# Routed adapters, two layers on one core: the first eviction ahead of h's transposes, and item 0 taken before the order of pairs is known

## The chip, the cores and the metric

One core of one Trainium2 chip. The metric is the device time of one execution in microseconds (us), as the median of several runs; a lower time is better. One further execution is recorded by the hardware profiler, and all rows come from it.

## What is computed

Two layers of the same form act on 128 items of 128 rows and 1024 columns (all fp32). Each item has a role, 1 or 2 of 3 possible, and the role picks the adapter, the same index in both layers:

```
h = x @ W_down[role] + b_down[role]      # 1024 -> 512
h = gelu(h)                              # exact
u = h @ W_up[role] + b_up[role]          # 512 -> 1024
y = x + u
out = (y - mean(y)) * rsqrt(var(y) + 1e-5) * gamma[role] + beta[role]
```

The output of layer 0 is the input of layer 1.

## The kernel before

**Order of the work.** The items are sorted by adapter (that of item 0 first) and taken two at a time, so a pair shares its weights. A layer has 65 pairs, the two layers 130, and the program counts them through. At the start VectorE computes the order of the items (`c_ord`), the adapter of each pair (`c_q`) and its kind (`c_kind`: 0, the same adapter as the pair before; 1 or 2, a new one) from the roles. `s_ctl` and `s_kind` tell the other engines that these are written.

**Arithmetic.** Each fp32 operand is split into a high part (type fp32r, a copy on ScalarE: `xh`, `wdh`, `wuh`, `hh`) and a low part (the difference, on VectorE: `xl`, `wdl`, `wul`, `hl`). A product is then three matmuls: high by high, high by low, low by high. The down product of an item is 8 x 3 matmuls into a bank `pD[e]`, e being the item of the pair. The up product of a pair is done on both items at once, by a scheme of seven half-size products (Strassen's) into the banks `bX` (two, in turn) and `bZ`. The combinations of h that it needs are GpSimd's `sums` (`cs`), those of the weights VectorE's `factors` and one more subtraction (L881).

**A step, software-pipelined.** In step i the engines work on pair i (down), w = i-2 (h of that pair is prepared) and u = i-3 (up product, evictions, the layer norm's sums); the norm's last parts and the store belong to i-4. TensorE's order in a step (L541 to L569) alternates: product 0 of u, a quarter of the down product of i, product 1, a quarter, and so on to product 6 and the last two quarters. Each product waits for the eviction of the bank that it adds to (`s_v`), for its weights (`s_wu`) and its half of h (`s_hl`). Product 2 waits for the first eviction of u.

An eviction on VectorE adds a bank to half an item's row tile in `xt` (`onto`, L943, the first three; `last_onto`, L951, the last four, which also sum the rows). ScalarE seeds each bank with the bias before the products add to it (`seed_d`, `seed_x`, `seed_z`) and applies gelu. h goes through DRAM (`store_h`, `load_h` on SP's queue), comes back in blocks as `hq` and is transposed in blocks of 32 by VectorE into `hT` (`transpose_h`, L918). In layer 1, x comes back from DRAM in the same manner (`transpose_x`, L904).

**Each engine's program** is a list of `begin(i)` and `end(i)`, written out for the first steps and those at a layer's change, and otherwise a loop over six steps whose body begins with `end(i-1)`, so the jump back lies between a `begin` and an `end`. Work that belongs to a new adapter stands in a conditional block (`kinds.when_new`, `when_near`, `when_far`), which is jumped over where the kind says so.

**VectorE's begin(i)** (L1004) is, in order: read of a kind, the two `transpose_h` of w, first eviction of u, with new down weights their second half of low parts (`take_wd_1`), low part of x of item 1 (`low_x`), second eviction, `low_h` 0, third eviction, with new up weights their last three low parts (`take_wu_2`), variance, the two `scale` (L974), fourth eviction, transpose of x, fifth eviction, with a new adapter for w the up bias (`bias`, L865), `low_x` of the next pair's item 0, sixth eviction, mean. **end(i)** (L1040) begins with `take_wu_0` (first two low parts of the up weights), `take_wd_0`, then the remaining `low_h`, the last eviction, and `take_wu_1`.

**ScalarE's end(i)** (L732) issues the loads of weights, then goes through high parts of h, the norm's scaling of u-1 (`normal`), `high_x` and gelu, `take_wu_0` (four high parts), the wait for the down bias (`bias_landed`), the seeds, `take_wd_0`, squares. The load of the down bias itself is SP's (`down_bias`, L301, L411), ahead of its row loads.

**At the start** SP issues the roles, item 0's x, and, once the first adapter is known, the down bias and four chunks of down weights (L392 to L398). ScalarE waits for `s_ctl` and `s_kind` (L577) before anything of item 0. TensorE zeroes the two `pD` banks, then computes sums for the order (L508), then zeroes `bX` and `bZ` (L511).

## Time and profile before

| | |
|---|---|
| runs | 2773.15, 2773.26, 2773.27 us; median 2773.26 |
| profiled execution | 2774.88 us, its span 2773.0 us |
| granted TensorE clock, mean | 0.991 |
| VectorE busy | 2179.8 us (79%) |
| ScalarE busy | 1667.0 us (60%) |
| GpSimd busy | 1382.2 us (50%) |
| DMA engines, mean busy share | some 6 tenths all through, 207 GB/s |
| chain that ended last | TensorE 83%, issue 7%, VectorE 6%, DMA, ScalarE, GpSimd 1% each |

The profile times every instruction of each engine, and names what ended an engine's idle time ("releaser"). "PE" is TensorE's matmul, "PEld" its weight load, "DVE" VectorE, "ACT" ScalarE, "POOL" GpSimd, "SPq" SyncE's queue, which issues most DMAs; "DVEq L895" is a semaphore that VectorE raises at line 895 (`ready`). "issue" stands for idle time in which nothing that the profile shows was awaited. Of a line that is merged from n instructions, the time is that of all n. Matmuls overlap: they start 0.227 us apart and are shown with 0.39.

### The profile page before, as it was taken

Reading aid. Unit: us, or ns where it says so; the run is one execution under the profiler, and the core shown is the slowest. Engines: PE = TensorE matmul, PEld = TensorE weight load, DVE = VectorE, ACT = ScalarE, POOL = GpSimd, SP = SyncE. Lnnn points to the kernel's source line nnn. Section 1 sums busy time; section 2 is a strip of 40 time slices with the busy share of each in tenths; the row PEclk is TensorE's granted clock in tenths of the full one; section 3 lists DMA queues with packets and bytes.
Section 4 is the critical chain, followed back from the end, with each engine's and each line's share of the span. In section 5 each row is a group of like instructions: output and inputs, shape, how many; then the busy total and the mean of one; then the engine's idle time right before and its main releaser. Section 6 shows DMA issues by size and latency. Waiting matters only on the chain.

```text
span 2773.0 us, 54757 instructions
## 1 busy us (share of the span) xinstructions
PE 2688.5 (97%) x11714; PEld 2204.8 (80%) x11714; DVE 2179.8 (79%) x3357; ACT 1667.0 (60%) x2905; POOL 1382.2 (50%) x1050
## 2 busy tenths in 40 slices
PE   8999999999999999999989999999889999999997
PEld 5888888877788888888768888888677888888885
DVE  6777777778777777777888788877788787878887
ACT  4666656666666666656666565665556565566565
POOL 1445555554555555555444454544444554544545
PEclk9999999999999999999999999999999999999999
DMA  6656666666666666666766665665756665666664
GB/s 207 212 200 213 211 204 208 205 223 226 211 213 204 207 208 207 209 204 238 232 190 198 200 220 191 212 208 188 240 178 214 198 218 193 209 207 198 206 208 149
DMA packets 360582, 573.29 MB, mean 207 GB/s; under 512 B 40144, under 2 KB 239952, under 8 KB 359248
## 3 DMA queue, kind: packets, MB, share of 16 engines
q1 hardware_dynamic: 359136, 554.92, 60.9%
q10 hardware_dynamic: 1008, 14.68, 1.4%
q14 instruction: 426, 3.49, 0.4%
q8 instruction: 12, 0.20, 0.0%
HBM read 364.97 MB, written 204.47 MB: 205 GB/s over the span
## 4 chain that ended last, share of the span: by engine, by line
PE 83%; issue 7%; DVE 6%; DMA 1%; ACT 1%; DVEq 1%; POOL 1%; SPq 0%; ACTq 0%; POOLq 0%
PE pD L524 44%; PE bX L536 23%; PE bZ L536 17%; DVE hl L933 1%; DVE xt L951 1%; DVE xT L904 1%; DVE wul L850 1%; DVE xt L943 1%; DVE wdl L831 0%; DMA htok<-hg 0%; DMA cbd<-in_bd 0%; DMA out<-xt 0%; DVEq L258 0%; SPq L387 0%; DVE hT L918 0%
## 5 line engine op out<-in xcount | busy, mean ns | idle before, releaser
L524 PE MATMUL pD<-wdh,xh 128*128 128x512 f32 x2080 | 812.4, 391 | 9.6 <-DVEq L895 9.6
L524 PE MATMUL pD<-wdl,xh 128*128 128x512 f32 x2080 | 811.4, 390 | 0.0
L524 PE MATMUL pD<-wdh,xl 128*128 128x512 f32 x2080 | 811.0, 390 | 0.0
L469 POOL TENSOR_TENSOR xt<-xt,cgb 128x1024 f32<-128x1024 f32 x258 | 620.7, 2406 | 370.4 <-ACT xt L717 370.4
L709 ACT ACTIVATE pC<-xt,nmean 128x512 f32<-128x512 f32 x520 | 358.6, 690 | 288.8 <-DVE nmean L959 280.1
L477 POOL TENSOR_TENSOR cs<-hT 128x256 f32<-128x256 f32 x130 | 97.5, 750 | 828.6 <-DVE hT L918 828.6
L717 ACT ACTIVATE xt<-xt,rstd 128x1024 f32<-128x1024 f32 x258 | 296.5, 1149 | 325.3 <-POOL rstd L455 321.7
L524 PEld LDWEIGHTS pD<-wdh,xh 128*128 128x128 f32 x2080 | 392.1, 189 | 94.0 <-DVEq L895 7.9
L536 PE MATMUL bX<-wuh,hh 128*128 128x512 f32 x1040 | 411.0, 395 | 49.9 <-DVE xt L943 41.5
L524 PEld LDWEIGHTS pD<-wdl,xh 128*128 128x128 f32 x2080 | 392.1, 189 | 81.7
L524 PEld LDWEIGHTS pD<-wdh,xl 128*128 128x128 f32 x2080 | 391.8, 188 | 81.9
L536 PE MATMUL bX<-wul,hh 128*128 128x512 f32 x1040 | 407.5, 392 | 0.0
L536 PE MATMUL bX<-wuh,hl 128*128 128x512 f32 x1040 | 407.3, 392 | 0.0
L933 DVE TENSOR_TENSOR hl<-cs,hh 128x512 fp32r<-128x512 f32 x260 | 287.3, 1124 | 148.1 <-issue 139.8
L699 ACT ACTIVATE hh<-cs 128x512 fp32r<-128x512 f32 x260 | 163.7, 630 | 350.0 <-PE bX L536 258.0
L974 DVE SCALAR_TENSOR_TENSOR xt<-xt,nmean,cgb 128x1024 f32<-128x1024 f32 x260 | 324.2, 1287 | 0.5 <-issue 0.3
L536 PE MATMUL bZ<-wuh,hh 128*128 128x512 f32 x780 | 304.6, 390 | 7.3 <-issue 5.0
L536 PE MATMUL bZ<-wul,hh 128*128 128x512 f32 x780 | 303.8, 389 | 0.0
L536 PE MATMUL bZ<-wuh,hl 128*128 128x512 f32 x780 | 303.7, 389 | 0.0
L452 POOL TENSOR_TENSOR rstd<-var,mhalf 128x2 f32<-128x2 f32 x129 | 218.4, 1693 | 164.2 <-DVE var L966 161.8
L536 PEld LDWEIGHTS bX<-wuh,hh 128*128 128x128 f32 x1040 | 196.5, 189 | 104.3 <-DVE xt L943 51.4
L951 DVE SCALAR_TENSOR_TENSOR xt<-bX,xt 128x512 f32<-128x512 f32 x260 | 177.2, 682 | 104.2 <-PE bX L536 102.7
(105 smaller groups left out, 3834.2 us busy)
## 6 DMA issues: line engine op xcount, KB each, us to landing
xq<-in_xB SPq DMA_DIRECT2D x130, 512.0 KB, 3.5
htok<-hg SPq DMA_DIRECT2D x260, 256.0 KB, 2.8
hq<-htok SPq DMA_DIRECT2D x1040, 64.0 KB, 2.2
xt<-in_x SPq DMA_DIRECT2D x130, 512.0 KB, 4.3
mid<-xt SPq DMA_DIRECT2D x130, 512.0 KB, 3.7
xq<-mid SPq DMA_DIRECT2D x520, 128.0 KB, 3.2
xt<-mid SPq DMA_DIRECT2D x130, 512.0 KB, 4.2
out<-xt SPq DMA_DIRECT2D x128, 512.0 KB, 2.9
```

Source lines behind the costliest of these rows:

```text
L452: eng.tensor_tensor(rstd[:, n:n + 2], var[:, n:n + 2], mhalf[:, 0:1].broadcast_to([128, 2]), ALU.pow)\
L469: eng.tensor_tensor(xt[:, k, :], xt[:, k, :], cgb[:, 1, :], ALU.add).then_inc(s_o, 1)
L477: eng.tensor_tensor(cs[:, 0, :], b1, b2, ALU.add).then_inc(s_S, 1)
L524: last = eng.matmul(pD[e][:, :], a[:, e, 128 * k:128 * k + 128], w[:, k, :], start=False, stop=(k == 7 and n == 2), skip_group_check=True)
L536: last = eng.matmul(bank[:, :], a[:, left, 128 * c:128 * c + 128], w[:, n, c, :], start=(start and c == 0 and m == 0), stop=(c == 1 and m ...
L699: eng.activation(dst, src, ACT.Copy).then_inc(s_hh, 1)
L709: eng.activation(junk[:, :], xt[:, u.slot(e), K * m:K * m + K], ACT.Square, bias=nmean[:, n:n + 1], accum_out=ssq[:, b, m, e:e + 1]).then_ ...
L717: eng.activation(xt[:, k, :], xt[:, k, :], ACT.Copy, scale=rstd[:, n:n + 1]).then_inc(s_z, 1)
L850: eng.tensor_tensor(wul[:, n, :, :], block, wuh[:, n, :, :].bitcast(fp32), ALU.subtract)\
L933: eng.tensor_tensor(blocks, src, high.bitcast(fp32), ALU.subtract).then_inc(s_hl, 1)
L951: eng.scalar_tensor_tensor(out=half(u, e, m), in0=bank[:, :], scalar=1.0, in1=half(u, e, m), op0=ALU.mult, op1=ALU.add, accum_out=ys[:, b, ...
L974: eng.scalar_tensor_tensor(out=xt[:, k, :], in0=xt[:, k, :], scalar=nmean[:, n:n + 1], in1=cgb[:, 0, :], op0=ALU.add, op1=ALU.mult).then_i ...
```

## The change

It moves work and leaves the arithmetic as it is:

- VectorE's `begin(i)`: the first eviction of u stands ahead of the two transposes of h, and the read of a kind behind the low part of x.
- VectorE's `take_wu_0` takes in `bias` and the subtraction that stood in `take_wu_1`. It is called in `begin(i)` where `bias` was, ahead of the low part of the next x and the sixth eviction, and no longer in `end(i)`.
- ScalarE's `take_wu_0` stands earlier in `end(i)`, ahead of `normal`, `high_x` and gelu.
- The load of a new down bias is issued by ScalarE at the head of `end(i)` and no longer by SP.
- Item 0: ScalarE takes its x, bias, seed and first two high parts of the weights ahead of its wait for the order; VectorE takes x's low part before it finishes the order; TensorE zeroes all banks ahead of its sums for the order.

```diff
--- before.py
+++ after.py
@@ -298,11 +298,6 @@
                 s = p.times(2, e - 2 * NP * p.layer())
                 return eng.value_load(c_ord[0:1, bass.ds(s, 1)], min_val=0, max_val=NB - 1)
 
-            def down_bias(p):
-                row = adapter(p)
-                count(eng, s_sd, p + -1, 2, 2)
-                eng.dma_start(cbd[:, :], bd[row, :].broadcast_to([128, K])).then_inc(s_bd, 16)
-
             def up_biases(p):
                 row = adapter(p)
                 count(eng, s_sz, p + -1, 1, 1)
@@ -407,8 +402,6 @@
                 store_h(v, 1)
                 load_blocks(i + 1, 1)
                 load_h(v, 1)
-                if not (i + 1).first():
-                    kinds.when_new(i + 1, down_bias)
                 load_rows(w, 0)
                 load_rows(w, 1)
                 store(z, 0)
@@ -504,13 +497,13 @@
             for bank in pD:
                 last = eng.matmul(bank[:, :], zero[:, 0:128], zero[:, 0:K], start=True, stop=True)
             last.then_inc(s_bits, 1)
+            for bank in bX + [bZ]:
+                last = eng.matmul(bank[:, :], zero[:, 0:128], zero[:, 0:K], start=True, stop=True)
+            last.then_inc(s_bits, 1)
             eng.wait_ge(s_oh, 2)
             eng.matmul(pC[0:1, 0:NSLOT], jf[:, :], oneh[:, :], start=True, stop=True)
             eng.matmul(pC[0:1, NSLOT:2 * NSLOT], rf[:, NB:NB + 1], oneh[:, :], start=False, stop=True,
                        skip_group_check=True).then_inc(s_pc, 1)
-            for bank in bX + [bZ]:
-                last = eng.matmul(bank[:, :], zero[:, 0:128], zero[:, 0:K], start=True, stop=True)
-            last.then_inc(s_bits, 1)
 
             def down(i, e, q):
                 if i.exists():
@@ -574,8 +567,6 @@
         def _(eng):
             eng.wait_ge(s_id, 2)
             eng.activation(gelu_set[:, :], mhalf[:, :], ACT.Gelu)
-            eng.wait_ge(s_ctl, 1)
-            eng.wait_ge(s_kind, 1)
             kinds = Kinds(eng, "ac_kind")
             fd = Phases(eng, "ac_fd", 1)
             fu = Phases(eng, "ac_fu", 1)
@@ -591,6 +582,11 @@
 
             def load_up(p):
                 fetch_up(eng, adapter(p), fu.next())
+
+            def load_bias(p):
+                row = adapter(p)
+                count(eng, s_sd, p + -1, 2, 2)
+                eng.dma_start(cbd[:, :], bd[row, :].broadcast_to([128, K])).then_inc(s_bd, 16)
 
             def bias_landed(p):
                 eng.wait_ge(s_bd, pb.next() * 16 + 16)
@@ -716,6 +712,14 @@
                     count(eng, s_n, p, 2, e + 1)
                     eng.activation(xt[:, k, :], xt[:, k, :], ACT.Copy, scale=rstd[:, n:n + 1]).then_inc(s_z, 1)
 
+
+            high_x(Pair(0), 0)
+            bias_landed(Pair(0))
+            seed_d(Pair(0), 0)
+            take_wd_0(Pair(0))
+            eng.wait_ge(s_ctl, 1)
+            eng.wait_ge(s_kind, 1)
+
             def begin(i):
                 kinds.read(i + 2)
                 kinds.when_new(i, take_wd_1)
@@ -731,23 +735,28 @@
 
             def end(i):
                 u, w = i + -3, i + -2
+                if not (i + 1).first():
+                    kinds.when_new(i + 1, load_bias)
                 kinds.when_near(w, load_up)
                 kinds.when_far(i, load_up)
                 kinds.when_near(i + 1, load_down)
                 kinds.when_far(i + 2, load_down)
                 high_h(w, 1)
+                if not w.first():
+                    kinds.when_new(w, take_wu_0)
                 normal(u + -1, 0)
-                high_x(i + 1, 0)
+                if not (i + 1).first():
+                    high_x(i + 1, 0)
                 gelu(i, 0)
                 high_h(w, 2)
-                if not w.first():
-                    kinds.when_new(w, take_wu_0)
-                kinds.when_new(i + 1, bias_landed)
-                seed_d(i + 1, 0)
+                if not (i + 1).first():
+                    kinds.when_new(i + 1, bias_landed)
+                    seed_d(i + 1, 0)
                 normal(u + -1, 1)
                 seed_x(w)
                 seed_z(w)
-                kinds.when_new(i + 1, take_wd_0)
+                if not (i + 1).first():
+                    kinds.when_new(i + 1, take_wd_0)
                 square(u, 0, 0)
                 square(u, 0, 1)
                 high_h(w, 3)
@@ -803,6 +812,11 @@
             link(eng.tensor_scalar(m1[:, :], io[:, 0:NSLOT], edge, par1, ALU.is_ge, ALU.mult))
             link(eng.tensor_tensor(m0[:, :], m0[:, :], m1[:, :], ALU.subtract))
             eng.tensor_scalar(oneh[:, :], m0[:, :], float(NB - 1), pos, ALU.min, ALU.is_equal).then_inc(s_oh, 1)
+
+            eng.wait_ge(s_xq[0], 16)
+            eng.wait_ge(s_xh, 1)
+            eng.tensor_tensor(xl[:, 0, :], xq[:, 0, :, :].rearrange("p b n -> p (b n)"), xh[:, 0, :].bitcast(fp32),
+                              ALU.subtract).then_inc(s_xl, 1)
             eng.wait_ge(s_pc, 1)
             heads = pC[0:1, NSLOT:2 * NSLOT].rearrange("p (n two) -> p n two", two=2)[:, :, 0]
             eng.tensor_copy(c_ord[:, :], pC[0:1, 0:NSLOT])
@@ -822,7 +836,6 @@
             kinds = Kinds(eng, "ve_kind")
             pd = [Phases(eng, f"ve_pd{g}") for g in range(2)]
             pt = Phases(eng, "ve_pt")
-            pb = Phases(eng, "ve_pb")
             pg = [Phases(eng, f"ve_pu{g}") for g in range(3)]
 
             def low_wd(c, q):
@@ -859,26 +872,23 @@
                 eng.wait_ge(s_sub, c * 4 + 2)
                 eng.tensor_tensor(t4, b21, t2, ALU.subtract).then_inc(s_sub, 1)
 
-            def bias(p):
-                c = pb.next()
+            def take_wu_0(p):
+                c = pg[0].next()
                 eng.wait_ge(s_bu, c * 16 + 16)
                 eng.tensor_tensor(cbu[:, K:H], cbu[:, K:H], cbu[:, 0:K], ALU.subtract).then_inc(s_bz, 1)
-                eng.wait_ge(s_bz, c + 1)
-                eng.sem_inc(s_seen, 1)
-
-            def take_wu_0(p):
-                c = pg[0].next()
                 low_wu(c * 7, 0, b11)
                 low_wu(c * 7, 1, b12)
+                eng.wait_ge(s_wul, c * 7 + 1)
+                eng.tensor_tensor(b11, t2, b11, ALU.subtract).then_inc(s_sub, 1)
                 eng.wait_ge(s_wul, c * 7 + 2)
+                eng.sem_inc(s_seen, 1)
+                eng.wait_ge(s_bz, c + 1)
                 eng.sem_inc(s_seen, 1)
 
             def take_wu_1(p):
                 c = pg[1].next()
                 low_wu(c * 7, 2, t2)
                 low_wu(c * 7, 3, b22)
-                eng.wait_ge(s_wul, c * 7 + 1)
-                eng.tensor_tensor(b11, t2, b11, ALU.subtract).then_inc(s_sub, 1)
                 eng.wait_ge(s_wul, c * 7 + 4)
                 eng.sem_inc(s_seen, 1)
 
@@ -1007,13 +1017,13 @@
                 if (u + -1).last():
                     last_rows(u + -1)
                     return
-                kinds.read(i + 1)
+                onto(u, 1, X, 0, 0)
                 transpose_h(w, 0)
                 transpose_h(w, 1)
-                onto(u, 1, X, 0, 0)
                 kinds.when_new(i, take_wd_1)
                 ready(i, s_wd[1])
                 low_x(i, 1)
+                kinds.read(i + 1)
                 onto(u, 2, bZ, 1, 1)
                 low_h(w, 0)
                 if u.last():
@@ -1031,9 +1041,11 @@
                 last_onto(u, 4, bZ, 0, 1, 3)
                 transpose_x(i + 1, 0)
                 last_onto(u, 5, X, 1, 1, 2)
-                kinds.when_new(w, bias)
+                kinds.when_new(w, take_wu_0)
                 ready(w, s_cb)
-                low_x(i + 1, 0)
+                ready(w, s_wu[0])
+                if not (i + 1).first():
+                    low_x(i + 1, 0)
                 last_onto(u, 6, bZ, 0, 0, 1)
                 mean(u, 0, 6)
 
@@ -1041,8 +1053,6 @@
                 u, w = i + -3, i + -2
                 if (u + -1).last():
                     return
-                kinds.when_new(w, take_wu_0)
-                ready(w, s_wu[0])
                 kinds.when_new(i + 1, take_wd_0)
                 ready(i + 1, s_wd[0])
                 if not only_up(i):
```

## Rows read from the trace of the kernel before

**Rows 1.** The page, part 1: busy time and instructions of each engine.
```profile
PE 2688.5 (97%) x11714; PEld 2204.8 (80%) x11714; DVE 2179.8 (79%) x3357; ACT 1667.0 (60%) x2905; POOL 1382.2 (50%) x1050
```

**Rows 2.** Waits of TensorE: line, for what; us in total, times, longest.
```profile
PE bX L536 <- DVE xt L943: 41.5, 21, 5.7
```

**Rows 3.** Timeline, an ordinary step of layer 0: start, us, engine, line, operation.
```profile
1136.73 0.39 PE L536 MATMUL bX<-wuh,hl 128*128 128x512 f32 x1
...
1136.38 1.30 DVE L918 STREAM_TRANSPOSE hT<-hq 128x512 f32<-128x512 f32 x2
...
1142.59 0.69 DVE L943 TENSOR_TENSOR xt<-bX,xt 128x512 f32<-128x512 f32 x1 [1.43 <-PE bX L536]
```

**Rows 4.** Timeline, a loop turn of layer 1 (VectorE), and TensorE's waits at turns.
```profile
2206.64 0.69 DVE L933 TENSOR_TENSOR hl<-cs,hh 128x512 fp32r<-128x512 f32 x1 [4.86 <-issue]
...
2211.29 1.30 DVE L918 STREAM_TRANSPOSE hT<-hq 128x512 f32<-128x512 f32 x2
...
2214.22 0.67 DVE L943 TENSOR_TENSOR xt<-bZ,xt 128x512 f32<-128x512 f32 x1
...
2213.22 0.50 PE L536 MATMUL bX<-wuh,hh 128*128 128x512 f32 x1 [1.29 <-DVE xt L943]
...
1567.36 0.50 PE L536 MATMUL bX<-wuh,hh 128*128 128x512 f32 x1 [1.29 <-DVE xt L943]
...
2585.50 0.50 PE L536 MATMUL bX<-wuh,hh 128*128 128x512 f32 x1 [1.05 <-DVE xt L943]
```

**Rows 5.** Timeline of the start, and landing of the first weights (by tile).
```profile
13.45 0.28 DVE L820 CUSTOM_DVE_ANT_0 c_kind<-c_new,c_near 1x260 uint16<-1x260 uint16 x1
...
14.97 1.06 ACT L651 ACTIVATE xh<-xq 128x1024 fp32r<-128x1024 f32 x1 [12.69 <-issue]
...
17.52 2.36 DVE L831 TENSOR_TENSOR wdl<-rwd,wdh 128x1024 fp32r<-128x1024 f32 x2 [0.24 <-ACT wdh L605]
...
20.18 0.76 PE L524 MATMUL pD<-wdh,xh 128*128 128x512 f32 x1 [3.69 <-DVEq L895]
...
DMA to landing us min/median/max: 4.5/5.6/6.7
```

**Rows 6.** Timeline, the first up weights.
```profile
52.77 1.23 DVE L911 TENSOR_TENSOR xl<-xq,xh 128x1024 fp32r<-128x1024 f32 x1 [2.92 <-ACT xh L651]
...
64.24 0.50 PE L536 MATMUL bX<-wuh,hh 128*128 128x512 f32 x1 [1.96 <-DVE xt L943]
```

**Rows 7.** Waits of ScalarE, then the timeline, new down weights in layer 1.
```profile
ACT pD L668 <- DMA cbd<-in_bd: 7.8, 2, 6.8
...
1972.37 0.39 PE L524 MATMUL pD<-wdh,xh 128*128 128x512 f32 x1
...
1979.71 2.65 DVE L831 TENSOR_TENSOR wdl<-rwd,wdh 128x1024 fp32r<-128x1024 f32 x2 [8.91 <-ACT wdh L605]
...
1992.44 0.51 PE L524 MATMUL pD<-wdh,xh 128*128 128x512 f32 x1 [1.49 <-DVEq L895]
```

**Rows 8.** Timeline of TensorE, new down weights at the change of layer.
```profile
1336.87 0.39 PE L524 MATMUL pD<-wdh,xh 128*128 128x512 f32 x1
...
1346.69 0.50 PE L536 MATMUL bX<-wuh,hh 128*128 128x512 f32 x1 [1.49 <-DVE xt L943]
...
1349.84 0.50 PE L524 MATMUL pD<-wdh,xh 128*128 128x512 f32 x1 [1.50 <-DVEq L895]
```

**Rows 9.** Timeline, new up weights; last, a stretch: us, PE busy, clock, DMA, GB/s.
```profile
1418.36 0.79 PE L536 MATMUL bX<-wuh,hh 128*128 128x512 f32 x1 [5.67 <-DVE xt L943]
...
1406.29 2.40 POOL L469 TENSOR_TENSOR xt<-xt,cgb 128x1024 f32<-128x1024 f32 x1 [5.54 <-ACT xt L717]
...
1406.68 2.57 DVE L933 TENSOR_TENSOR hl<-cs,hh 128x512 fp32r<-128x512 f32 x1 [0.63 <-DVE wul L850]
...
2035.00:2040.00 5.00, 4.61 (x13) 0.66 0.64 196
```

**Rows 10.** Waits of VectorE: idle time before the low halves of h.
```profile
DVE hl L933 <- issue: 205.5, 244, 5.1
```

## The prediction

> **What bounds the kernel now.** I read the page first: TensorE is busy for 97% of the span [rows 1], so only its idle time, some clock loss and what lies before its first real matmul can be won. The waits come next. Of TensorE's own waits nearly all lie behind one line, the first kind of eviction, VectorE's add of a bank into xt at L943: 41.5 us in 21 waits [rows 2]. The timeline then shows where they are, and they fall into three kinds.
>
> The ordinary step has none. In layer 0 the last matmul of product 0 starts at 1136.73, VectorE begins the two transposes of h at 1136.38, and it still idles 1.43 us before its third eviction [rows 3]. A change in that step is worth nothing.
>
> The loop turns of layer 1 are the second kind. VectorE stands still for 4.86 us at the jump back ("issue": nothing that the profile shows is awaited), comes late to the transposes at 2211.29, spends 1.30 us on them and only then does the first eviction, for which TensorE has waited 1.29 us at 2213.22. The same wait is there at eight turns, from 1567.36 to 2585.50; they add up to 9.8 us [rows 4].
>
> The third kind are the start and the steps in which an adapter changes [rows 5 to 9].
>
> **Loop turns.** The change puts the first eviction ahead of the transposes. Its bank is ready long before (product 0 is two groups of matmuls earlier), so at a turn it starts where the transposes did and ends about 2211.3 + 0.67 = 2212.0, when TensorE has just come to it (2213.22 - 1.29 = 2211.9). What is late next is the second eviction: transposes, low half of x and eviction together end where they did, at 2214.22 + 0.67 = 2214.9, and TensorE, coming 12 matmuls (2.9 us) after 2211.9, meets it within 0.1 us [rows 4]. So 8 x (1.2 - 0.1) or **-9.0 us**; the ends are 0 and -9.8. The transposes themselves become later by one eviction, 0.7 us, in layer 1. In layer 0 VectorE arrives 0.35 us before product 0's last matmul has even started, so it waits some 0.8 us and the transposes are 1.5 us later; the 1.43 us of idle time before the third eviction, with smaller idle times before it, take that up [rows 3]. GpSimd's sums, ScalarE's high halves and SP's loads of hq wait for the transposes and slide by the same 0.7 to 1.5 us; all of them are needed only a step later. Cost of the move in the ordinary step: nothing, by this cover.
>
> **Start.** Before, ScalarE takes item 0's x only after the order of pairs: that order is written at 13.45 + 0.28, and the first high half starts at 14.97, 1.24 us on. Bias, weights' high halves and x's low half follow, VectorE's low halves of the weights run 17.52 to 19.88, and TensorE starts at 20.18, 0.30 us behind [rows 5]. After, x, bias and the first two high halves are done while the order is still being worked out; the four weight loads, which SP issues as soon as the first adapter is known, take 4.5 to 6.7 us, and I take the first two chunks as landed when the order is done. VectorE does x's low half before the order is finished (it delays that by 0.1 to 0.3 us) and comes to the weights when the order is done, at 13.9 plus its own entry into the program. I take ScalarE's 1.24 us for that entry: 15.0 + 2.36 + 0.30 = 17.7, or **-2.5 us**. Ends: entry in no time, -3.7; only x's low half saved (1.23 us, [rows 6]), -1.2. The three banks zeroed earlier on TensorE fill time in which it only waited. The first real matmul took 0.76 us against 0.39 later [rows 5, 7], so the clock was low there; it stays so, since an idle stretch precedes it again.
>
> **First up weights.** VectorE now does the first half of pair 0's up weights right behind the bias, in the stretch where it idled 2.92 us before x's low half at 52.77 [rows 6]. The chain from there to the first eviction, for which TensorE waited 1.96 us at 64.24, and on to the last three parts is VectorE's own. It ends 2.9 us sooner: **-2.9 us**, ends 0 and -2.9.
>
> **Middle of layer 1, new down weights.** SP issued the bias late in its queue, and ScalarE waited for it: 7.8 us in two waits, 6.8 of them here [rows 7]. ScalarE's high halves of the weights stood behind, and VectorE idled 8.91 us until 1979.71. Now ScalarE issues the load itself at the head of its half step, some 7 us before the seed needs it; weight loads of twice its size took 4.5 to 6.7 [rows 5]. The 6.8 us are gone. From the matmuls behind product 6 to the third group of down matmuls it took 1992.44 - 1972.37 = 20.1 us here, and 1349.84 - 1336.87 = 13.0 at the change of layer, where the bias was on time [rows 7, 8]. The difference, 7.1, holds some clock loss. I take **-6.6 us**, ends 0 and -7.1. The other wait, 1.0 us in the middle of layer 0, gives **-0.7 us**, since the last seed behind it waits for VectorE anyway; ends 0 and -1.
>
> **Down weights elsewhere.** At the change of layer TensorE waited 1.49 us for the first eviction and 1.50 for the weights' second half [rows 8]. The eviction now comes in time, but the weights' low halves end where they did, so the second wait grows to 3.0: **0 us**. A single idle stretch of that length can cost clock. In 2035 to 2040, behind an idle stretch of 2.5, the granted clock was 0.66 [rows 9], a loss of some 1.6 us. Two steps get such a stretch, and I count one of them: **+1.6 us**, ends 0 and +3.2.
>
> **Up weights (three steps).** TensorE waits up to 5.67 us for VectorE's chain [rows 9]. The chain gets shorter by the transposes (1.3 us). But the first half of the up weights (bias, two low halves, one subtraction) now stands beside GpSimd's two shifts. GpSimd's add from 1406.29 takes 2.40, and VectorE's subtraction of 512 columns issued at 1406.68 takes 2.57 instead of 0.69 [rows 4, 9]: it waited for GpSimd to end. Before, such a block cost this chain 1.9 us once or so; now both shifts lie across it, up to 4.8. The Trainium skill, "SBUF — State Buffer", section "SBUF: two separate sides", says that a VectorE operation with two SBUF inputs and a GpSimd operation exclude each other for a whole instruction; by it alone the step would cost about 2 us more at each of the three. ScalarE's early high halves of the weights also put off x's high half, so that TensorE meets it late, inside a chain that VectorE bounds anyway. I take -0.6 at each, **-1.8 us** in all; ends -3.9 and +6.
>
> **Tail.** The first eviction once leaves the transposes behind, but the rest of the chain stays: **-0.3 us**.
>
> **Sum.** -9.0 - 2.5 - 2.9 - 6.6 - 0.7 + 1.6 - 1.8 - 0.3 = -22.2 us against the profiled execution's 2774.88 (span 2773.0, 1.9 around it): 2752.7. The median of the runs lies 1.6 lower, so 2751.
>
> **Rivals.** (1) *Turns and start only.* The switches are chains of VectorE, ScalarE and GpSimd together; what is won at one point may come back at the next, with the clock down each time. Then -9.0 - 2.5 - 2.9 + 3.2 = -11.2 remain, 2762. For it: the blocks of rows 9. Against it: ScalarE's wait for the bias is named by the profile and has no second cause. (2) *More is won.* All waits at the turns, the start at its near end, the up steps at theirs and no clock loss: -9.8 - 3.7 - 2.9 - 7.1 - 1.0 - 3.9 - 0.3 = -28.7, 2745. (3) *A stall of instruction supply, slower.* A conditional block of five operations is now skipped in the middle of VectorE's begin instead of at the head of end. If that skip stalls once a turn as the jump back does, in the same step, there is no slack under it: 4.86 - 0.6 (an ordinary one) = 4.3 us at some ten turns of layer 1, +43 against -22, so 2794. Below half that price it does not decide. Against it: 244 such idle times add up to 205.5 us, 0.84 on average with the turns among them [rows 10], so skips of blocks as long cost about 0.6. The Trainium skill, "Runtime: NRT & Kernel Launch", section "Instruction fetch mechanics", says that a taken branch whose target lies outside the fetched window stalls; the 4.86 us at the turn fit that. (4) *No change.* If the first eviction still comes late, because something else (product 0, or the stall growing) holds VectorE at the turn, and the bias lands no sooner, only the 5 us of start and first weights remain: 2768.
>
> **Chances.** Forecast 0.6; (1) 0.19; (2) 0.12; (3) 0.04; (4) 0.05. A difference of 0.2%, 5.5 us, is about what a measurement tells from none. Faster by more: 0.91; within: 0.05; slower: 0.04. The range reaches from rival 2 to rival 1, with their margins: 2743 to 2762.
>
> **What would show it.** At the layer 1 turns: first eviction ahead of the transposes, and no wait of 1.1 to 1.3 us at product 2. TensorE's first real matmul at about 17.7. No wait of ScalarE for cbd, and VectorE's low halves in the middle of layer 1 about 6 us sooner. At the up steps the wait of about 5 us split in two, with GpSimd's adds between VectorE's low halves. Wrong would be: the waits at the turns still over 1 us, a VectorE idle time over 1 us at the new skip, or an ordinary step that takes longer than before.

## The result, and the profile after

The kernel after the change takes 2748.98 us (median of 4 runs, 2748.43 to 2749.48) against 2773.2 of the kernel before (4 runs in the same comparison, 2772.51 to 2773.27): the ratio is 0.9913, 95% interval 0.9896 to 0.993. The profiled execution took 2748.52 us, its span is 2746.7, against 2774.88 and 2773.0. The forecast was 2751.0, with a range of 2743 to 2762.

Part 1 of the page of the kernel after, to be read beside [rows 1]:

```profile
PE 2686.8 (98%) x11714; PEld 2207.3 (80%) x11714; DVE 2209.5 (80%) x3357; ACT 1669.8 (61%) x2905; POOL 1388.9 (51%) x1050
```

TensorE's busy time is 1.7 us less, and the span is 26.3 less: idle time went. VectorE is busy 29.7 us longer with as many instructions, some of them drawn out. The waits of the kernel after (engine, tile, line, what was awaited: us in total, times, longest):

```profile
DVE hl L943 <- issue: 161.8, 243, 4.5
...
PE pD L517 <- DVEq L905: 18.9, 7, 5.6
...
PE bX L529 <- DVE xt L953: 8.2, 7, 2.2
PE bX L529 <- DVEq L905: 8.1, 4, 2.5
PE bZ L529 <- issue: 7.6, 4, 3.2
...
ACT pD L664 <- DMA cbd<-in_bd: 3.2, 1, 3.2
```

The first eviction, now L953, kept TensorE waiting 41.5 us in 21 waits [rows 2]; now 8.2 in 7. Part of that came back elsewhere. TensorE's waits for VectorE's low parts ahead of `pD` were these in the kernel before:

```profile
PE pD L524 <- DVEq L895: 9.6, 5, 3.7
```

They are now 18.9 us. The longest is the one at the start in both kernels, 3.7 before and 5.6 now, where TensorE is only ready sooner. ScalarE waits for the down bias once, at the start, instead of the 7.8 us of [rows 7]. The sum called issue was 205.5 [rows 10] and is 161.8; the forecast had not expected that.

The timeline of the kernel after, at the start, the first up weights, the up weights of layer 1, the middle of layer 1, a turn and the last steps (start, us, engine, line, operation):

```profile
13.52 0.28 DVE L834 CUSTOM_DVE_ANT_0 c_kind<-c_new,c_near 1x260 uint16<-1x260 uint16 x1
...
14.42 2.36 DVE L844 TENSOR_TENSOR wdl<-rwd,wdh 128x1024 fp32r<-128x1024 f32 x2 [0.61 <-DVE c_kind L834]
...
17.08 0.76 PE L517 MATMUL pD<-wdh,xh 128*128 128x512 f32 x1 [5.57 <-DVEq L905]
...
60.56 2.89 DVE L863 TENSOR_TENSOR wul<-rwu,wuh 128x1024 fp32r<-128x1024 f32 x2
...
62.33 1.71 POOL L475 TENSOR_TENSOR cs<-hT,cs 128x256 f32<-128x256 f32 x1
...
63.37 1.75 DVE L863 TENSOR_TENSOR wul<-twu,wuh 128x1024 fp32r<-128x1024 f32 x1
...
65.43 0.47 PE L529 MATMUL bX<-wuh,hh 128*128 128x512 f32 x1 [2.51 <-DVEq L905]
...
1393.41 6.82 POOL L462 TENSOR_TENSOR xt<-xt,cgb 128x1024 f32<-128x1024 f32 x2 [2.83 <-ACT xt L713]
...
1393.42 4.56 DVE L863 TENSOR_TENSOR wul<-rwu,wuh 128x1024 fp32r<-128x1024 f32 x2
1397.90 3.42 DVE L882 TENSOR_TENSOR rwu<-twu,rwu 128x1024 f32<-128x1024 f32 x1
...
1403.46 0.50 PE L517 MATMUL pD<-wdh,xh 128*128 128x512 f32 x1 [2.80 <-DVEq L905]
...
1411.07 0.50 PE L529 MATMUL bX<-wuh,hh 128*128 128x512 f32 x1 [1.65 <-DVE xt L953]
...
1958.97 2.69 DVE L844 TENSOR_TENSOR wdl<-rwd,wdh 128x1024 fp32r<-128x1024 f32 x2 [2.47 <-ACT wdh L601]
...
1971.29 0.49 PE L517 MATMUL pD<-wdh,xh 128*128 128x512 f32 x1 [2.47 <-DVEq L905]
...
2182.75 0.69 DVE L943 TENSOR_TENSOR hl<-cs,hh 128x512 fp32r<-128x512 f32 x1 [4.49 <-issue]
...
2187.17 0.68 DVE L953 TENSOR_TENSOR xt<-bX,xt 128x512 f32<-128x512 f32 x1
2187.77 1.29 DVE L928 STREAM_TRANSPOSE hT<-hq 128x512 f32<-128x512 f32 x2
...
2694.96 0.69 DVE L953 TENSOR_TENSOR xt<-bX,xt 128x512 f32<-128x512 f32 x1 [2.08 <-PE bX L529]
...
2719.01 0.76 PE L529 MATMUL bZ<-wuh,hh 128*128 128x512 f32 x1 [3.16 <-issue]
```

Stretches of the kernel after (window, us, busy time and count of each engine, granted clock, DMA share, GB/s):

```profile
65.40:69.90 4.50, 4.47 (x13) 3.58 (x14) 2.27 (x5) 1.64 (x3) 0.00 (x0) 0.62 0.90 269
...
1342.00:1346.00 4.00, 4.00 (x11) 3.13 (x12) 3.97 (x7) 0.64 (x2) 2.82 (x4) 0.57 0.77 222
...
1403.40:1407.40 4.00, 3.94 (x10) 3.13 (x11) 3.54 (x7) 3.08 (x7) 0.00 (x0) 0.57 0.05 18
...
1971.30:1976.00 4.70, 4.36 (x18) 3.29 (x19) 4.59 (x7) 0.63 (x1) 3.45 (x4) 1.00 0.89 274
...
2719.00:2724.60 5.60, 5.59 (x13) 4.43 (x14) 2.23 (x7) 3.14 (x6) 4.12 (x2) 0.50 0.24 97
```

Both kernels issue the same matmuls, so the same matmul can be looked up in both traces. How much earlier or later it starts, taken from one place to the next, is what each place won or lost:

| place | forecast | measured |
|---|---|---|
| start | -2.5 | -3.7 |
| first up weights | -2.9 | -0.65 |
| middle of layer 0, down weights | -0.7 | -1.8 |
| middle of layer 0, up weights | -0.6 | -0.9 |
| change of layer, down weights | 0 and clock +1.6 | +0.2 |
| layer 1, first up weights | -0.6 | -0.7 |
| eight turns of layer 1 | -9.0 | -12.9 |
| middle of layer 1, down weights | -6.6 | -6.7 |
| middle of layer 1, up weights | -0.6 | -2.4 |
| last steps | -0.3 | +2.8 |
| sum | -22.2 | -26.8 |

(The forecast's last term for the up weights, -1.8, is split over its three steps. Of the span's 26.3 us 0.4 is rounding and the very end.)

### The profile page after: what moved, and what is told of

The parts are those of the page before. It is cut to its first block, busy times and chain, and to the rows that moved or that the text cites. A ratio compares the mean times of both kernels' runs of the same rounds, so it can differ in the third digit from the quotient of the medians.

```text
span 2746.7 us, 54496 instructions
## 1 busy us (share of the span) xinstructions
PE 2686.8 (98%) x11714; PEld 2207.3 (80%) x11714; DVE 2209.5 (80%) x3357; ACT 1669.8 (61%) x2905; POOL 1388.9 (51%) x1050
## 4 chain that ended last, share of the span: by engine, by line
PE 88%; DVE 6%; issue 4%; ACT 1%; DVEq 1%; POOL 0%; DMA 0%; ACTq 0%; POOLq 0%; SPq 0%
PE pD L517 47%; PE bX L529 23%; PE bZ L529 18%; DVE wul L863 1%; DVE xt L961 1%; DVE hl L943 1%; DVE xT L914 1%; DVE wdl L844 0%; DVE xt L953 0%; DVE xl L921 0%; DVE hT L928 0%; DVE xt L984 0%; ACT wdh L601 0%; ACT pC L705 0%; DMA xt<-in_itok 0%
## 5 line engine op out<-in xcount | busy, mean ns | idle before, releaser
L517 PE MATMUL pD<-wdh,xh 128*128 128x512 f32 x2080 | 813.2, 391 | 18.9 <-DVEq L905 18.9
L462 POOL TENSOR_TENSOR xt<-xt,cgb 128x1024 f32<-128x1024 f32 x258 | 629.1, 2439 | 348.7 <-ACT xt L713 348.7
L470 POOL TENSOR_TENSOR cs<-hT 128x256 f32<-128x256 f32 x130 | 154.0, 1185 | 907.4 <-DVE hT L928 907.4
L943 DVE TENSOR_TENSOR hl<-cs,hh 128x512 fp32r<-128x512 f32 x260 | 302.9, 1184 | 103.4 <-issue 96.8
L953 DVE TENSOR_TENSOR xt<-bX,xt 128x512 f32<-128x512 f32 x260 | 178.9, 688 | 149.6 <-PE bX L529 147.1
```

Source lines behind the costliest of these rows:

```text
L462: eng.tensor_tensor(xt[:, k, :], xt[:, k, :], cgb[:, 1, :], ALU.add).then_inc(s_o, 1)
L470: eng.tensor_tensor(cs[:, 0, :], b1, b2, ALU.add).then_inc(s_S, 1)
L517: last = eng.matmul(pD[e][:, :], a[:, e, 128 * k:128 * k + 128], w[:, k, :], start=False, stop=(k == 7 and n == 2), skip_group_check=True)
L943: eng.tensor_tensor(blocks, src, high.bitcast(fp32), ALU.subtract).then_inc(s_hl, 1)
L953: eng.tensor_tensor(half(u, e, m), bank[:, :], half(u, e, m), ALU.add).then_inc(s_v, 1)
```

## The experiments

### One part undone at a time

**e1_undo_evict.** The first eviction stands behind the two transposes again:

```diff
-                onto(u, 1, X, 0, 0)
                 transpose_h(w, 0)
                 transpose_h(w, 1)
+                onto(u, 1, X, 0, 0)
```

> The changed kernel with one edit: the first eviction stands behind the transposes of h again. Theory (the eviction's place carries the loop turns): the eight waits of 1.1 to 1.3 us for the first eviction at the turns of layer 1 are back, and cost with TensorE's restart some 1.6 us each, 13 us; single waits at steps with a new adapter add 1 to 4; the tail gives 2.8 back. About 2761 to 2765, against 2749 for the changed kernel. Rival (the turns were won by the block of up weights that left the head of the half step behind the jump back): the turns stay without waits, 2749 to 2753.

Measured: 2755.96 us (2753.35 to 2756.6), ratio 0.994 [0.9924, 0.9957]; that is 7.0 above the kernel after, between the two expectations. Its timeline:

```profile
1398.19 1.22 DVE L882 TENSOR_TENSOR rwu<-twu,rwu 128x1024 f32<-128x1024 f32 x1
...
1398.25 3.40 POOL L462 TENSOR_TENSOR xt<-xt,cgb 128x1024 f32<-128x1024 f32 x1 [1.07 <-ACT xt L713]
...
1410.59 0.50 PE L529 MATMUL bX<-wuh,hh 128*128 128x512 f32 x1 [4.64 <-DVE xt L953]
...
1557.65 0.50 PE L529 MATMUL bX<-wuh,hh 128*128 128x512 f32 x1 [1.38 <-DVE xt L953]
```

The waits at all eight turns are back. Matmul by matmul it loses 5.3 us on the kernel after over the first four turns (1421 to 1929) and 6.8 from 2061 to 2563; of these, 5.0 belong to the other four turns, and the rest to a wait of 2.32 behind the new up weights (2067.29). It loses 2.2 in the middle of layer 0. But it wins 1.2 at the first up weights, 3.4 and 3.6 where layer 1 takes new up weights, and 2.3 in the last steps. (The execution in this trace was the fastest of the four, 4.8 us above the profiled one of the kernel after.) The L882 row shows why at one of these: there the subtraction takes 1.22 us and GpSimd's second add starts behind it (3.40 long); with the eviction first, GpSimd's two adds follow each other without a gap (6.82 for both) and the same subtraction takes 3.42. Moving one eviction changed which of the two engines came first.

**e2_undo_bias.** SP issues the down bias again (`down_bias`, with `kinds.when_new(i + 1, down_bias)` ahead of `load_rows`), ScalarE's `load_bias` is gone.

> The changed kernel with one edit: SP issues the load of a new down bias again, ahead of its row loads. Theory: ScalarE waits again some 7 us for cbd in the middle of layer 1 and 1 us in the middle of layer 0, of which 6.6 and 0.7 reach TensorE: about 2756. Rival (VectorE's chain there is as long anyway, since the eviction and the up weights moved too): 2749 to 2751.

Measured: 2758.75 us (2756.81 to 2762.63), ratio 0.9947 [0.9931, 0.9964], 9.8 above the kernel after. From its timeline:

```profile
1328.58 0.60 ACT L671 ACTIVATE pD<-cbd 128x512 f32<-128x512 f32 x1 [2.47 <-DMA cbd<-in_bd]
...
1968.42 0.60 ACT L671 ACTIVATE pD<-cbd 128x512 f32<-128x512 f32 x1 [8.60 <-DMA cbd<-in_bd]
...
1970.67 0.77 PE L536 MATMUL bX<-wuh,hh 128*128 128x512 f32 x1 [6.07 <-issue]
```

ScalarE's wait is back, longer than the 6.8 of [rows 7], and TensorE's with it. So the load's late issue is the cause of that wait. Matmul by matmul this run loses 9.3 us on the kernel after in the middle of layer 1, where the change had won 6.7 and where ScalarE's wait is now 1.8 us longer than before the change. It loses 2.7 at the change of layer, where a new wait of 2.47 stands (1328.58). In the middle of layer 0 it loses nothing: there the bias lands in time here too. So this run says nothing on the 1.8 us that the change won there. It also loses 2.3 us over the eight turns, although VectorE's program is the same as in the kernel after. (The execution in this trace was the slowest of the four, 14.1 us above the profiled one of the kernel after, where the medians are 9.8 apart.)

**e3_undo_start.** Item 0's x is taken behind the order of pairs again, on all three engines (`eng.wait_ge(s_ctl, 1)`, `eng.wait_ge(s_kind, 1)` ahead of ScalarE's first work, no early `xl`, the last three banks zeroed behind the sums for the order).

> The changed kernel with the start undone: ScalarE waits for the order before item 0, VectorE takes the low half of its x after the order, TensorE zeroes the last three banks after its sums for the order. Theory: TensorE's first real matmul is at 20.2 instead of 17.1, and all the rest is shifted by that and no more: about 2752.5. Rival (the first up weights set the end of this stretch whatever the start): 2749 to 2750, with a shorter wait for the first up weights.

Measured: 2752.73 us (2750.59 to 2753.42), ratio 0.9929 [0.9912, 0.9945], 3.7 above the kernel after: the time that was expected. In its trace the first real matmul starts at 19.43 and not at the 20.2 expected, 2.35 later than 17.08. (That execution took 2750.59 us, the shortest of the four, and is only 2.1 us above the profiled one of the kernel after.)

**e4_undo_wu.** VectorE's `bias` and `take_wu_0` are two blocks again, the second at the head of `end(i)`, the subtraction is back in `take_wu_1`, and ScalarE's `take_wu_0` stands behind `high_h` 2.

> The changed kernel with the first half of the up weights put back on both engines (bias alone in begin, the two low halves at the head of end, the subtraction with the second half; ScalarE's four high halves behind the high half of h). Theory (locks between GpSimd's shifts and VectorE cost what the shorter chain gives): 2747 to 2751, VectorE's subtraction without the 3.4 us of the changed kernel. Rival A (the new place is worth the 2 to 3 us by which the shift grew at these steps): 2752 to 2755. Rival B (the new place only costs): under 2746.

Measured: 2753.01 us (2751.87 to 2754.09), ratio 0.9928 [0.9911, 0.9944], 4.0 above the kernel after: rival A. The waits of VectorE in it:

```profile
DVE hl L947 <- issue: 206.6, 243, 5.2
```

That is the sum of the kernel before. Matmul by matmul against the kernel after, it loses 2.0 us from 1421 to 1932 and 1.3 from 2070 to 2565, stretches that hold turns and no new weights at all (its trace is 5.6 us longer in sum). This led to the runs with a block added or taken away below.

The four parts undone cost 7.0 + 9.8 + 3.7 + 4.0 = 24.5 us together, against 24.2 that the change brought. That they add up so well is partly chance, as the next run shows.

**b1_evict_only.** The kernel before, with the eviction (and the read of a kind) moved and nothing else.

> The kernel before with one part of the change alone: the first eviction ahead of the two transposes of h, and the read of the next item's kind behind the low half of x. Theory (the eviction's 12.9 us at the eight turns of the loop are its own, and it gives back some 6 us in the tail, at the change of layer and at the first up weights, since undoing it in the kernel after cost only 7 us): 5 to 9 us below the kernel before, 2764 to 2768. Rival (its loss at the weights came only together with the moved low parts, so alone it wins the whole of the turns): 11 to 14 us below, 2759 to 2762.

Measured: 2768.16 us (11 runs, 2764.33 to 2772.25) against 2773.34 (15 runs), ratio 0.9981 [0.9971, 0.999]: 5.2 us won, at the lower end of the theory. Its timeline:

```profile
1561.78 0.69 DVE L933 TENSOR_TENSOR hl<-cs,hh 128x512 fp32r<-128x512 f32 x1 [4.83 <-issue]
```

Its eight turns give 8.6 us against the kernel before, the 9.0 of the forecast to 0.4. The rest of the 12.9 goes with VectorE's idle time at the turns (here 4.4 to 5.2 us in layer 1, 4.90 on average at the eight; in the kernel after 4.06 to 4.49, 4.30 on average). It gives back some 2 us up to the first steps of layer 1, where TensorE now also waits at turns of layer 0 (204.75, 450.63 and 954.27, 0.57 to 0.79 us), and 2.5 in the last steps.

### Can the rest be had?

**c1_tail.** In the last steps, those without down products, the transposes come first:

```diff
-                onto(u, 1, X, 0, 0)
+                if not only_up(i):
+                    onto(u, 1, X, 0, 0)
                 transpose_h(w, 0)
                 transpose_h(w, 1)
+                if only_up(i):
+                    onto(u, 1, X, 0, 0)
```

> The kernel after the change, with the first eviction again behind the two transposes in the last steps alone, those in which no down product is left. In the trace of the kernel after the change TensorE loses 2.8 us more in those steps than before the change (3.16 at 2703.68 and again 3.16 at 2719.01, with a low clock behind the second). Theory (VectorE waits there for product 0, whose eviction now stands ahead of the transposes of h, and so hands the halves of h over late): the two waits of 3.16 go back to those of the kernel before, and the time is some 2.8 us below the kernel after, 2746 to 2747. Rival (the tail is late by the up weights and by GELU, whatever VectorE's order): the waits stay and the time stays at 2748.5 to 2749.5.

Measured: 2747.76 us (2747.16 to 2748.72), ratio 0.9907 [0.9892, 0.9922], 1.2 below the kernel after. In the timeline:

```profile
2703.06 0.47 PE L529 MATMUL bZ<-wuh,hh 128*128 128x512 f32 x1 [1.84 <-issue]
...
2711.84 0.50 PE L529 MATMUL bX<-wuh,hh 128*128 128x512 f32 x1 [3.09 <-DVE xt L953]
```

The waits of 3.16 are 1.84 (as before the change) and 1.21, so VectorE's order was their cause; but a new one of 3.09 for the first eviction stands between them, with a low clock behind it (1.46 there in the kernel before). Matmul by matmul 2.0 of the 2.8 came back; by the medians of the runs 1.2, which is about the scatter.

**c2_wd.** As c1_tail, and `take_wd_1` ahead of the transposes, behind the first eviction.

> As c1_tail, and in the other steps VectorE's take_wd_1 (the second part of the down weights' low parts, only in steps with new weights) stands ahead of the two transposes of h and behind the first eviction. Theory (the low parts of the new down weights end last before TensorE's wait at the change of layer, 2.47 at 1342.00, and before the waits in the middle of the layers, and the transposes of h have time there): the three waits shrink by the 1.3 us that two transposes take on VectorE, the clock does not fall behind the first of them, and the time is 3 to 5 us below c1_tail, 2741 to 2744. Rival (the transposes of h are as urgent as the low parts, since h's product follows): what the weights win h loses, and the time is within 1 us of c1_tail or above it, 2746 to 2748.

Measured: 2746.72 us (2745.87 to 2749.26), ratio 0.9905 [0.989, 0.992]: within 1.1 of c1_tail, so the rival. In the timeline:

```profile
1342.20 0.50 PE L517 MATMUL pD<-wdh,xh 128*128 128x512 f32 x1 [1.76 <-DVEq L905]
...
1345.40 0.50 PE L529 MATMUL bZ<-wuh,hh 128*128 128x512 f32 x1 [1.54 <-DVE xt L953]
```

The wait for the weights shrank from 2.45 to 1.76, and 1.54 came up one product on. One chain of VectorE feeds both.

**c3_lowx.** As c1_tail, and `low_x(i + 1, 0)` ahead of `take_wu_0`.

> As c1_tail, and on VectorE the low half of x for the next item's first down product stands ahead of the low parts of the first up weights (take_wu_0) instead of behind them, which matters in the three steps with new up weights. Theory (TensorE's waits of 1.8, 2.8 and 2.8 us at 673.6, 1403.5 and 2032.2 are for that low half, which is queued behind a subtraction that the shared port draws out to 3.4 us): these waits go, the up weights' own waits behind them grow by less, and the time is 2 to 5 us below c1_tail, 2742 to 2744. Rival (VectorE's work before the first up product is one chain, so what goes at the first wait comes back at the next): the wait moves from the low half to the up weights and the time is that of c1_tail, within 1.5 us.

Measured: 2748.27 us (2747.27 to 2749.28), ratio 0.9908 [0.9892, 0.9923]: nothing, the rival. In the timeline:

```profile
1403.42 1.21 DVE L882 TENSOR_TENSOR rwu<-twu,rwu 128x1024 f32<-128x1024 f32 x1
...
1404.52 0.50 PE L529 MATMUL bX<-wuh,hh 128*128 128x512 f32 x1 [2.69 <-ACT bX L672]
```

The wait of 2.80 for a down product is gone, one of 2.69 stands at the up product before it: ScalarE's seed of `bX` needs the up bias, which `take_wu_0` makes, now 1.2 us later. Even the subtraction at its undisturbed 1.21 us did not help.

### What a block that is jumped over costs

**d1_extra.** The kernel after with one more conditional block at the head of `end(i)`:

```diff
+            def spare(p):
+                eng.sem_inc(s_seen, 1)
...
+                if not w.first():
+                    kinds.when_new(w, spare)
                 kinds.when_new(i + 1, take_wd_0)
```

> The kernel after the change, with one more conditional block on VectorE at the head of its end(i), where the first low parts of the up weights stood before; what it holds is one count on a semaphore that nobody waits for, and it is jumped over in all but the three steps with new up weights. Reason for it: VectorE's idle time ahead of the low halves of h that the profile calls issue is 205 to 212 us in the three kernels that have such a block there (before, eviction alone, up weights undone) and 162 to 167 in the seven that have not. Theory (a block that is jumped over costs VectorE 0.33 us in each of 130 steps, and at the loop's turns, where it is late, TensorE pays for it): that idle time goes back to 205 to 210, the turns of layer 1 lose 2.5 to 3 us together, and the time is 2751 to 2752.5; the 4 us that undoing the up weights cost were then mostly this block and not the place of the weights. Rival (the difference is what the place of the weights costs): idle time 162 to 170, time 2748.5 to 2749.5.

Measured: 2767.67 us (11 runs, 2765.25 to 2770.23), ratio 0.9977 [0.9968, 0.9986]: 18.7 us slower than the kernel after, against 2.5 to 3 expected. A waits row, then two rows of the timeline:

```profile
DVE hl L943 <- issue: 225.7, 245, 6.9
```

```profile
1559.61 0.69 DVE L943 TENSOR_TENSOR hl<-cs,hh 128x512 fp32r<-128x512 f32 x1 [6.39 <-issue]
...
1564.76 0.50 PE L529 MATMUL bX<-wuh,hh 128*128 128x512 f32 x1 [0.92 <-DVE xt L953]
```

The sum did rise (by 64 us), so the rival is out. In ordinary steps the block costs what was expected: the second of two idle times per step is 0.52 us instead of 0.25 (ahead of the low halves of h the kernel after has 121 idle times near 0.52 and 95 near 0.25, this one 206 near 0.52). But at the turns of layer 1 the idle time is 5.8 to 6.4 us instead of 4.06 to 4.49, and the first eviction is late again at each. Matmul by matmul the eight turns lose 15.9 us on the kernel after, most of the cost.

**d4_mid.** The same block, in the middle of `end(i)`, ahead of its `last_onto`.

> The kernel after the change with the same additional block as in the run d1_extra (one count on a semaphore, jumped over in nearly all steps), but in the middle of VectorE's end(i), behind low_h 2 and ahead of the last eviction, instead of at its head, where the loop jumps back to. In d1_extra it cost 18.7 us: VectorE's idle time at a turn rose from 4.48 to 6.39 us and in the other steps by 0.3. Theory (what is dear is the place right behind the jump back, where one more jump comes on top of the stall; elsewhere it costs the 0.3 of a skip): the idle time at the turns stays at 4.3 to 4.8, the sum of VectorE's idle time called issue rises by 35 to 45 us, and the time is 2748.5 to 2752. Rival (it is the length of the loop's body, or that block itself, wherever it stands): turns of 6 us or more and 2762 to 2768.

Measured: 2762.02 us (2761.17 to 2764.51), ratio 0.9961 [0.9948, 0.9975], 13.0 above the kernel after. The waits, then the timeline:

```profile
DVE hl L943 <- issue: 168.2, 241, 6.1
```

```profile
2191.30 0.69 DVE L943 TENSOR_TENSOR hl<-cs,hh 128x512 fp32r<-128x512 f32 x1 [6.14 <-issue]
...
2196.45 0.50 PE L529 MATMUL bX<-wuh,hh 128*128 128x512 f32 x1 [0.93 <-DVE xt L953]
```

In ordinary steps it does not show: ahead of the low halves of h there are 110 idle times near 0.51 and 104 near 0.25, about as in the kernel after. The block stands ahead of an eviction for whose bank VectorE often waits anyway, which would hide it. The turns are nearly as dear as in d1_extra: 5.6 to 6.2 us in layer 1. So my theory falls: it is not the place behind the jump back. The rival holds as far as this pair goes: a further block somewhere in the loop's body makes the jump back dearer. What of it (the number of instructions, where the body's ends come to lie) stays open: the kernel before, e4_undo_wu and b1_evict_only have a block more as well, and their idle times at those turns are 4.4 to 5.2, not 6. Nor does VectorE's own program settle the idle time: e2_undo_bias has that of the kernel after, and at the eight turns it idles 4.64 us on average instead of 4.30.

**d2_nest.** The last two blocks of `end(i)` share one outer condition:

```diff
-                kinds.when_far(i + -1, factors)
-                kinds.when_new(w, take_wu_1)
+                def both():
+                    kinds.when_far(i + -1, factors)
+                    kinds.when_new(w, take_wu_1)
+
+                kinds.when_any(i + -1, w, both)
                 ready(w, s_wu[1])
```

> The kernel after the change, with VectorE's last two conditional blocks of end(i) (the far factors and take_wu_1) put inside one outer block whose condition is the sum of the two kinds, so that an ordinary step jumps once instead of twice. Theory (each jump costs 0.33 us in each of 130 steps): VectorE's idle time called issue falls by some 40 us in total over its rows, and where TensorE still waits for VectorE (the turns, 0.1 to 0.2 each, and the last steps) a little is won, 0 to 1.5 us: 2747.5 to 2749. Rival A (what costs is not the jump but the reading of a kind into the condition, of which the outer block needs two): no idle time is saved and the time stays at 2749 or rises. Rival B (the longer jump stalls the supply of instructions): idle time grows, 2752 or more.

Measured: 2748.15 us (2747.63 to 2748.7), ratio 0.9911 [0.9896, 0.9926], 0.8 below the kernel after, as the theory has it and within scatter. Its waits:

```profile
DVE hl L954 <- issue: 139.1, 244, 4.7
```

The sum fell by 22.7 us, not 40: nearly all idle times ahead of the low halves of h are now near 0.28 (206 of them), so the outer condition seems to have its own cost.

**d3_both.** c1_tail, with this nest and a second one around `take_wu_2` and the near `factors`.

> The best version that the runs point to: the eviction behind the transposes in the last steps only, the nested block of the run before, and a second one around take_wu_2 and the near factors in begin(i). Theory: two jumps fewer in each of 130 steps, some 80 us of VectorE's idle time called issue gone, the tail at its earlier order; 2745.5 to 2747. Rival (TensorE is bound nearly everywhere now, so idle time of VectorE won is worth nothing): the time of the kernel with the tail's order alone, 2747.8, within 1 us.

Measured: 2745.43 us (2742.93 to 2746.65), ratio 0.9898 [0.9883, 0.9913]: the fastest of all, 3.6 below the kernel after. Its waits:

```profile
DVE hl L954 <- issue: 117.1, 239, 4.7
```

The time is inside the theory's 2745.5 to 2747 but for 0.1, and 2.3 below c1_tail. Its own runs lie up to 3.7 us apart, so that it beats the kernel after is likely, and its exact lead is not known.

## Why the prediction was right, point by point

**Turns: right in mechanism, term too small.** The eviction starts where the transposes did (2187.17, transposes behind it), and TensorE's wait is gone. Eviction alone gives 8.6 (b1_evict_only) where I had 9.0. (A slip in the working did not matter: 12 matmuls at 0.227 us are 2.7 us, not 2.9, and TensorE meets the second eviction without a wait all the same.) The end of -9.8 was the counted idle time, but the matmuls' own distances lose 12.0 us at these turns. The other 4 us come with a part that the forecast priced at nothing: `bias` and `take_wu_0` became one block, so VectorE jumps once less in each of 130 steps. 205.5 - 161.8 = 43.7 us, 0.34 a step, and at the eight turns 4.30 us on average instead of 4.76. Undoing that part (e4_undo_wu) costs 3.3 us at the turns. That it is the number of blocks which shortens the turns is not shown: one block more in d1_extra and d4_mid costs far more than this, and e2_undo_bias, with the same program on VectorE, wins 10.7 us at the turns instead of 12.9. I had [rows 10] before me and used them only for a rival in which the skip costs something; that one block fewer wins something was not drawn from them. The Trainium skill, "Advanced Engine Details and Errata", section "Control Flow Timing", gives about 108 ns for a compare-and-branch; the 0.34 us that a block costs here is three times that, so a skipped block is more than its branch.

**The stall rival (3).** It did not happen: no idle time over 1 us appeared at the skip in `begin`, and the turn became shorter. A cost of that kind exists all the same, at the jump back: with one block more VectorE idles 5.6 to 6.4 us there, and the kernel takes 13.0 and 18.7 us longer. What the Trainium skill says in "Runtime: NRT & Kernel Launch", section "Instruction fetch mechanics", that a taken branch to a target outside the fetched pages stalls, fits the turns and not the skips; no run here shows the fetch itself.

**Start: -3.7 for -2.5.** I added 1.24 us for VectorE's entry behind the order; the row shows 0.61 (wdl at 14.42). The first matmul came at 17.08, 3.1 us sooner, where I had 17.7. A further 0.6 us came because the clock rose some matmuls sooner.

**First up weights: -0.65 for -2.9; the term that failed most.** The matmul that started at 64.24 [rows 6] starts at 57.32, 6.9 us sooner and 3.2 more than the start had won; 1.0 of that is the eviction's new place ahead of the transposes. VectorE's chain itself, up to the last low parts, runs 5.9 us sooner, so it won 2.2 of the 2.9. Most of the missing 0.7 is the last low part, which now runs beside a sum of GpSimd. Before, it ran alone (the two ahead of it were drawn out already):

```profile
67.02 2.88 DVE L850 TENSOR_TENSOR wul<-rwu,wuh 128x1024 fp32r<-128x1024 f32 x2
69.83 1.21 DVE L850 TENSOR_TENSOR wul<-twu,wuh 128x1024 fp32r<-128x1024 f32 x1
```

Now it takes 1.75 (63.37), beside 1.71 for a sum that takes 0.7 undisturbed. The larger loss is the clock. Before, TensorE waited 1.96 us at 64.24 and 1.36 at 71.35, with work between; now it waits 2.51 us in one piece for the low parts (65.43), the granted clock from there to 69.9 is 0.62, and another 1.6 us go. The step of the forecast that failed is "it ends 2.9 us sooner" taken as TensorE's gain: a clock loss behind the longer single wait had no term here. e1_undo_evict, with a wait of only 1.34 there, keeps its clock and is 1.2 us ahead at that point.

**Middle of layer 1, down weights: -6.7 for -6.6.** The bias was the cause (e2_undo_bias). VectorE's low parts start at 1958.97 instead of [rows 7]'s 1979.71. The 20.1 us became 13, the stretch at the change of layer.

**Down weights elsewhere: +0.2.** As forecast the two waits at the change of layer became one, 2.47 at 1342.00, and the clock fell behind it (0.57 from 1342 to 1346). In the middle of layer 1 the same single wait of 2.47, at 1971.29, left it at 1.00. So one of two such steps lost clock, as I had counted; nothing I had could tell which. In the middle of layer 0 the gain was 1.8 where I had 0.7 for the bias. ScalarE's wait of 1.0 is gone; b1_evict_only, in which nothing but the eviction and the read of a kind moved, wins 0.7 there, and the rest is not taken apart.

**Up weights.** -0.9, -0.7, -2.4 for -0.6 each. The collision with GpSimd that I bounded at +6 in all is there: 3.42 for a subtraction of 1.22, 4.56 for two low parts that take 2.34, so 4.4 us at the step of 1393 where it was 1.9 [rows 9]. The Trainium skill's rule that I had set beside it ("SBUF — State Buffer", section "SBUF: two separate sides") made it about 2 us more a step; the trace agrees, with 2.5. That the step still wins lies in the wait of 5.67 [rows 9], which fell apart into 2.80, 1.65 and 2.15, work running between.

**Last steps: +2.8 for -0.3; wrong sign.** I took the cover of layer 0's ordinary step for the tail. There no down product stands between the up products, so TensorE comes to product 0 late: VectorE idles 2.08 us (2694.96) ahead of the eviction where, before, it was doing the transposes. c1_tail shows the cause and gets 2.0 of it back in its trace, 1.2 by the medians.

**The clock and the numbers.** I had +1.6 us for the clock, in one place. It fell in several (65.4 to 69.9 at 0.62, 1403 to 1407 at 0.57, 2719 to 2724.6 at 0.50), but it had done so before the change too, and the mean granted clock rose from 0.991 to 0.992. So in all the clock did not cost what I had put down for it; it only lay elsewhere. The errors of the terms (-1.2, +2.25, -1.1, -0.3, -1.4, -0.1, -3.9, -0.1, -1.8, +3.1) sum to -4.6 of 26.8. The forecast of the time came out nearer, 2751 for 2748.98, partly by luck: large errors of opposite sign cancel (-3.9 at the turns, +2.25 at the first up weights, +3.1 in the last steps), and the profiled execution before was 1.7 us above its median where the one after is 0.5 below, so that the traces lie further apart than the medians.

## What to carry to other kernels

An operation whose input is ready goes ahead of one that feeds only the next step, but look at each regime of the loop by itself: in the last steps, where other work is missing between the products, the same order was wrong. A conditional block is not free when it is jumped over; on an engine that is late at the loop's turn, where its blocks stand and how many there are can matter as much as the order of its work: one block more cost 13 and 19 us here, more than any single part of the change won. Measure such a kernel after every edit, even one that adds nothing to the work. When work is moved beside another engine that can draw it out, take its duration from a stretch where both are running.

## What the runs showed that was not expected

- One more conditional block with a single semaphore count in it, jumped over in nearly every step, cost 18.7 us (0.7%) at the head of VectorE's `end`, and 13.0 in its middle. VectorE's idle time at the turns of layer 1 went from 4.06 to 4.49 us up to 5.6 to 6.4.
- A jump over a block costs VectorE 0.3 us where it waits for nothing else (idle times of 0.25 and 0.52 with one and two blocks between two operations).
- The length of a wait did not settle whether TensorE's clock fell. At the change of layer two waits of 1.14 and 1.49 us with work between (e1_undo_evict, 1340.00 and 1343.16) left the granted clock at 1.00 from 1340 to 1346; one wait of 2.47 (the kernel after, 1342.00) was followed by 0.57 from 1342 to 1346, nearer to the 1.2 GHz level than to the 2.4. But a wait of the same 2.47 at 1971.29 in the same trace was followed by 1.00. Where layer 0 takes new up weights in its middle, a wait of 2.25 was followed by 0.50 over 3 us in the kernel after (680.26) and by 1.00 in e2_undo_bias (680.10). What decides it is open.
- Waits cost TensorE's pace about 0.3 us each beyond the idle time that the profile counts: at the turns of the kernel before the counted idle time is 9.8 us, the matmuls' own distances lose 12.0. About half of it is the way of counting, since a matmul is shown with 0.39 us while the next one starts 0.227 behind it.
